# Decoder layer on one core: attention probabilities packed into 128-column tiles, normalization, clip, mask and q copies moved off VectorE, and a new order of steps

## The chip, the cores and the metric

The kernel runs on one core of one Trainium2 chip. The metric is the device time of one execution in microseconds (us). Single instructions are given in us or, where a row says so, in ns. The engines are TensorE (PE, with its weight loads as PEld), VectorE (DVE), ScalarE (ACT), GpSimd (POOL) and SyncE (SP, here only the queue that issues DMAs).

## What is computed

One pre-norm decoder layer for 32 batch rows of 256 tokens with 256 features. Three blocks follow one another, each with a LayerNorm ahead of it and a residual add behind it.

```
x = x + attn(layernorm(x))     # gated slot attention: short convolutions, rope on q and k,
                               # two causal passes with cumulative logsumexp weights
x = x + xattn(layernorm(x), ctx, mask)
x = x + ffn(layernorm(x))      # 8 experts of width 64, top 2, SwiGLU, all experts computed

# xattn: 16 heads of 16 features, 77 context positions
scores = jnp.einsum('bhqd,bhkd->bhqk', Q, K) / scale
scores = jnp.where(mask, scores, NEG_INF)
attention = jax.nn.softmax(scores, axis=-1)
heads_out = jnp.einsum('bhqk,bhkd->bhqd', attention, V)
```

## The kernel before

**Pipeline over batch rows.** A step of the loop works on four batch rows at once: `N` on the newest row (projections, convolution and gates of attn), `A` on the one before (the two passes and the output of attn), `X` on the next (xattn) and `F` on the oldest (ffn). 35 steps bring 32 rows through; names begin with `a_`, `x_` or `f_` by block. Steps 5 and on are an instruction loop of two steps a turn, since most buffers exist twice, by the parity of the row.

**Order.** Every engine has its own list of the parts of a step, written out by hand in `body`, and runs it strictly in order. Parts wait on one semaphore for each result (`on.x_prob`, `on.x_pT` and so on), so an engine stands still at the first part whose operands are late, with all behind it. `A1`, `X0` and the like are names of eight PSUM banks; `E0` carries everything of the projections, `X0` scores and projections of xattn, `X1` transposed probabilities, `X2` the output of the multiply with V.

**Numbers in halves.** Most multiplies take each operand as a rounded part and a remainder (`hi`, `lo`) and are three matmuls. Those of the probabilities, of V, of E and of the small states take four-byte data in one statement, which TensorE runs as two load and multiply pairs.

**xattn.** A row has two chunks of 128 tokens (`c`), and a chunk four groups of four heads (`q`), eight units `u` in all. For each: `x_s` writes scores of 4 x 77 columns to `X0` from block-diagonal masked copies of K (`K_bd`, `KT_lo_bd`, built by GpSimd in `x_kbd`) and adds the mask by a third matmul; `x_soft` on VectorE takes the maximum; `x_prob` on ScalarE makes four exponentials into `prob`; `x_pt` on TensorE transposes them, four 128x77 tiles; `x_pt` on ScalarE copies the result to `probT`; `x_av` multiplies each head's 77x128 tile with V and a column of ones (`Vx`, 17 columns a head), whose product with the probabilities is the denominator. `x_o` divides.

**Normalization.** `norm_stats` on VectorE (statistics of two 128x256 tiles, a `hold`, aggregation, plus epsilon), `rstd` on GpSimd (power -0.5), `norm_apply` on VectorE (subtract, multiply). A `hold` is an operation on one column whose result nobody uses; it stands between an operation and one that reads its result.

**DMA.** The sync queue stores the oldest row, then loads x, the context and the mask for new rows, four DMAs a step; each waits in queue order.

## Time and profile before

| | |
|---|---|
| three runs, us | 1811.38, 1815.34, 1818.04; median 1815.34 |
| span of the profiled execution | 1817.2 us |
| its TensorE clock | 0.981 of full speed |
| TensorE, its weight loads | 1666.7 us (92%), 1497.1 us (82%) |
| VectorE | 1496.2 us (82%) |
| ScalarE | 889.4 us (49%) |
| GpSimd | 774.7 us (43%) |
| HBM traffic | 13 GB/s over the span |

The span runs from the first to the last instruction of the one execution that was profiled; no other time of that execution is reported, so its span stands for it. Busy times are sums over the whole span. They say how much an engine has to do, not what a step waits for; the waits and the chain say that. Lengths of matmuls in a timeline overlap by their pipelines, so the cost of one is read from the start of one group to the start of the next.

### The profile page before, as it was taken

Reading aid. Unit: us, or ns where it says so; the run is one execution under the profiler, and the core shown is the slowest. Engines: PE = TensorE matmul, PEld = TensorE weight load, DVE = VectorE, ACT = ScalarE, POOL = GpSimd, SP = SyncE. Lnnn points to the kernel's source line nnn. Section 1 sums busy time; section 2 is a strip of 40 time slices with the busy share of each in tenths; the row PEclk is TensorE's granted clock in tenths of the full one; section 3 lists DMA queues with packets and bytes.
Section 4 is the critical chain, followed back from the end, with each engine's and each line's share of the span. In section 5 each row is a group of like instructions: output and inputs, shape, how many; then the busy total and the mean of one; then the engine's idle time right before and its main releaser. Section 6 shows DMA issues by size and latency. Waiting matters only on the chain.

```text
span 1817.2 us, 36129 instructions
## 1 busy us (share of the span) xinstructions
PE 1666.7 (92%) x12064; PEld 1497.1 (82%) x12064; DVE 1496.2 (82%) x3540; ACT 889.4 (49%) x2351; POOL 774.7 (43%) x809
## 2 busy tenths in 40 slices
PE   3699999999999999999999999999999999999986
PEld 3588888889888888888888988888888888898875
DVE  4778888888888888888888888888888888888652
ACT  2255544455554455555445555444555444555441
POOL 2344444444544444444444454444444444445320
PEclk9899999999999999999999999999999999999887
DMA  4000000000000000000000000000000000000000
GB/s 113 9 9 1 15 15 15 14 14 0 14 14 14 14 14 14 0 14 14 14 14 14 12 2 14 14 14 14 14 0 14 14 14 14 14 10 5 9 7 12
DMA packets 44572, 24.99 MB, mean 14 GB/s; under 512 B 24432, under 2 KB 44528, under 8 KB 44528
## 3 DMA queue, kind: packets, MB, share of 16 engines
q1 hardware_dynamic: 44528, 24.43, 5.1%
q8 instruction: 25, 0.41, 0.1%
q14 instruction: 19, 0.16, 0.0%
HBM read 16.03 MB, written 8.39 MB: 13 GB/s over the span
## 4 chain that ended last, share of the span: by engine, by line
PE 56%; DVE 30%; issue 9%; ACT 4%; DVEq 0%; DMA 0%; SPq 0%; POOL 0%; ACTq 0%; POOLq 0%
PE bank L377 49%; DVE a_conv L809 6%; PE bank L611 4%; DVE x_nmax L942 3%; DVE dve_scrap L252 2%; DVE a_xn L759 2%; PE bank L383 2%; DVE f_xn L759 2%; ACT x_prob L1211 2%; DVE a_E L792 1%; DVE a_stats L746 1%; DVE x_stats L746 1%; DVE f_s L1018 1%; DVE f_th L1013 1%; DVE x_xnT_lo L774 1%
## 5 line engine op out<-in xcount | busy, mean ns | idle before, releaser
L1211 ACT ACTIVATE x_prob<-bank,x_nmax 128x77 f32<-128x77 f32 x1024 | 247.7, 327 | 167.9 <-DVE x_nmax L942 163.7
L377 PEld LDWEIGHTS bank<-x_Vx,x_probT 77*128 77x128 f32 x2048 | 251.6, 193 | 2.9
L377 PE MATMUL bank<-x_Vx,x_probT 77*128 77x17 f32 x2048 | 246.2, 255 | 0.0
L1222 ACT ACTIVATE x_probT<-bank 77x512 f32<-77x512 f32 x256 | 152.4, 595 | 92.0 <-PE bank L611 92.0
L942 DVE TENSOR_REDUCE x_nmax<-bank 128x4 f32<-128x308 f32 x256 | 121.3, 474 | 59.8 <-PE bank L377 58.4
L611 PE MATMUL bank<-ident,x_prob 128*77 128x128 f32 x1024 | 155.9, 275 | 0.4 <-ACT x_probT L1222 0.4
L809 DVE SCALAR_TENSOR_TENSOR a_conv<-a_raw,cw,a_conv 128x256 f32<-128x256 f32 x384 | 156.2, 477 | 0.0
L1306 POOL TENSOR_TENSOR x_rstd<-x_ve,mhalf 128x2 f32<-128x2 f32 x32 | 22.6, 706 | 301.2 <-DVE x_ve L752 301.2
L1330 POOL TENSOR_TENSOR a_Er_lo<-a_E,a_Er_hi 128x512 fp32r<-128x512 f32 x32 | 74.2, 2320 | 142.2 <-ACT a_Er_hi L1114 142.2
L611 PEld LDWEIGHTS bank<-ident,x_prob 128*77 128x77 f32 x1024 | 124.0, 148 | 7.6 <-issue 0.6
L377 PE MATMUL bank<-x_K_bd,x_Q_stack 128*128 128x308 f32 x256 | 98.6, 385 | 15.0 <-ACT x_prob L1211 12.3
L841 DVE RECIPROCAL a_rC<-bank 128x512 f32<-128x512 f32 x32 | 107.1, 3348 | 0.3 <-PE bank L377 0.3
L1355 POOL TENSOR_TENSOR a_okn<-a_okn,a_okmax 128x512 f32<-128x512 f32 x32 | 33.4, 1043 | 165.0 <-DVE a_okmax L860 165.0
L1377 POOL TENSOR_TENSOR x_K_bd<-x_K_stack,groupmask 128x308 fp32r<-128x308 f32 x128 | 95.1, 771 | 17.5 <-DVE x_KT_lo L916 17.5
L1395 POOL TENSOR_TENSOR f_s<-f_s,f_wt 128x512 f32<-128x512 f32 x64 | 66.8, 1044 | 69.4 <-DVE f_s L1018 69.4
L252 DVE TENSOR_TENSOR dve_scrap<-mhalf 128x1 f32<-128x1 f32 x192 | 83.3, 434 | 5.5
L844 DVE TENSOR_TENSOR a_AT<-bank,tri 128x512 f32<-128x512 f32 x128 | 84.6, 680 | 2.4 <-PE bank L377 2.4
L1363 POOL TENSOR_TENSOR a_orinv<-a_ove,mhalf 128x8 f32<-128x8 f32 x32 | 52.7, 1647 | 79.1 <-DVE a_ove L878 79.1
L1137 ACT ACTIVATE a_ET<-bank 128x512 f32<-128x512 f32 x32 | 19.1, 597 | 133.4 <-PE bank L383 133.4
L1200 ACT ACTIVATE x_Q_stack<-bank 64x512 fp32r<-64x512 f32 x64 | 37.9, 592 | 86.3 <-PE bank L377 85.9
L377 PE MATMUL bank<-x_negmask,ident_bf 128*128 128x308 bf16 x256 | 79.5, 311 | 0.0
L377 PE MATMUL bank<-fwo_hi,f_sT_hi 128*128 128x256 f32 x256 | 76.7, 300 | 1.5 <-ACT f_sT_hi L1251 1.5
(250 smaller groups left out, 5585.2 us busy)
## 6 DMA issues: line engine op xcount, KB each, us to landing
x<-in_x SPq DMA_DIRECT2D x32, 256.0 KB, 2.9
out<-x SPq DMA_DIRECT2D x32, 256.0 KB, 2.2
ctxT<-in_ctxT SPq DMA_DIRECT2D x32, 77.0 KB, 2.5
keep<-in_mask SPq DMA_DIRECT2D x32, 19.2 KB, 2.6
f_s<-in_fWu SPq DMA_DIRECT2D x2, 256.0 KB, 5.6
a_AT<-in_Wv SPq DMA_DIRECT2D x1, 256.0 KB, 3.8
a_okn<-in_Ws SPq DMA_DIRECT2D x1, 256.0 KB, 3.9
a_qn<-in_Wg SPq DMA_DIRECT2D x1, 256.0 KB, 3.8
```

What stands on the lines that cost most here:

```text
L252: eng.tensor_tensor(scrap[:], mhalf[:, 0:1], mhalf[:, 0:1], ALU.mult)
L377: return pe.matmul(out, lhsT, rhs, start=start, stop=stop, skip_group_check=True)
L611: ins = pe.transpose(X1[0:S2, i * P:(i + 1) * P], prob[:, u % 2, i, :], ident[:])
L759: ins = ts(xn[s][:, c, :], src[:, c, :], ln_mv[s][:, c, 0:1], ln_rstd[s][:, c:c + 1], ALU.subtract, ALU.mult)
L809: stt(conv[:, j, :], raw[:, j, i:i + T], cw[:, j, i:i + 1], conv[:, j, :], ALU.mult, ALU.add).then_inc(on.a_conv, 1)
L841: dve.reciprocal(flat(rC[r.parity]), E0[:, :]).then_inc(on.a_rC, 1)
L844: return tt(dst, src.rearrange("p (h t) -> p h t", h=H), tri.rearrange("p (o t) -> p o t", o=1).broadcast_to([P, H, P]), ALU.mult)
L942: dve.tensor_reduce(nmax[:, u % 2, :], X0[:, 0:UH * S2].rearrange("p (h s) -> p h s", h=UH), AX.X, ALU.min).then_inc(on.x_max, 1)
L1211: ins = act.activation(prob[:, u % 2, i, :], X0[:, i * S2:(i + 1) * S2], ACT.Exp, scale=-1.0, bias=nmax[:, u % 2, i:i + 1])
L1222: act.activation(probT[:, u % 2].rearrange("p h t -> p (h t)"), X1[0:S2, :], ACT.Copy).then_inc(on.x_pT, 1)
L1330: pool.tensor_tensor(E_halves[1][:], E[r.parity][:], E_halves[0][:].bitcast(F32), ALU.subtract).then_inc(on.a_Elo, 1)
L1377: pool.tensor_tensor(K_bd[:, q], K_stack[:, q:q + 1, :].bitcast(F32).broadcast_to([P, UH, S2]), spread(groupmask[:], S2), ALU.mult)
```

## The change

**Probabilities packed.** `prob` becomes one array of 16 heads with a pitch of 80 columns, 1280 columns, the three between heads zero. A chunk's 1280 columns are ten tiles of 128, in groups of 2, 3, 2 and 3 tiles as heads become ready (`GROUPS`). Transposes, copies and the multiply work on tiles. V is laid out in blocks to fit (`Vbd`, two of them, 128 x 10 x 51): the rows of a tile belong to two or three heads, and each head has its own 17 columns, with zeros and the ones loaded once. The products add up in one PSUM bank.

```diff
-                for i in range(UH):
-                    ins = pe.transpose(X1[0:S2, i * P:(i + 1) * P], prob[:, u % 2, i, :], ident[:])
+                for i, t in enumerate(GROUPS[u % QU]):
+                    ins = pe.transpose(X1[:, i * P:(i + 1) * P], prob[:, t * P:(t + 1) * P], ident[:])
...
+                    pe.wait_ge(vbd_in, upto(r, V_DMAS))
...
-                for i in range(UH):
-                    h = q * UH + i
-                    ins = mm(X2[:, h * (HD + 1):(h + 1) * (HD + 1)], probT[:, u % 2, i, :], Vx[:, h, :])
+                for t in GROUPS[q]:
+                    h, w = first_head(t) * (HD + 1), tile_heads(t) * (HD + 1)
+                    ins = mm(X2[:, h:h + w], probT[:, t, :], Vbd[r.parity][:, t, 0:w], start=(t == 0),
+                             stop=(t == NT - 1))
```

**V spread by DMA.** ScalarE's `x_v` writes V to `Vtok` (77 x 16 x 16), and the sync queue copies it to its places in `Vbd`, twelve DMAs a row, behind the loads of a step and ahead of the store.

```diff
+            def spread_v(r):
+                sp.wait_ge(on.x_v, upto(r))
+                if second(r):
+                    sp.wait_ge(on.x_av_ps, upto(two_before(r), NU))
+                dst, src = Vbd[r.parity], Vtok[:].rearrange("s (g h) e -> s g h e", g=2)
+                for s, n, h, t, p, col in V_PIECES:
+                    sp.dma_start(dst[p:p + n, t::NT // 2, col:col + HD], src[s:s + n, :, h, :]).then_inc(vbd_in, 16)
```

**Work moved off VectorE.** `norm_apply` becomes two ScalarE activations that scale by `rstd` and add a shift; VectorE makes the negated mean, GpSimd the shift. The clip of the scores ahead of the exponential becomes one behind it, on GpSimd, in place. The mask (`negmask`) is made by GpSimd behind `x_kbd`, the four q copies (`a_qbd`) by ScalarE.

```diff
+                for c in range(TC):
+                    ins = act.activation(xn[s][:, c, :], src[:, c, :], ACT.Identity,
+                                         scale=ln_rstd[s][:, c:c + 1], bias=ln_shift[s][:, c:c + 1])
...
+                pool.wait_ge(on.rstd[s], upto(r))
+                pool.tensor_tensor(ln_shift[s][:], ln_neg[s][:], ln_rstd[s][:], ALU.mult).then_inc(on.shift[s], 1)
...
+            def a_clip(r):
+                pool.wait_ge(on.a_Eraw, upto(r))
+                hold_pool(pool, 1)
+                e = E[r.parity][:].rearrange("p c d -> p (c d)")
+                pool.tensor_scalar(e, e, E_MIN, E_MAX, ALU.max, ALU.min).then_inc(on.a_E, 1)
```

**Other forms of small operations.** A `hold` on VectorE and four small operations become `scalar_tensor_tensor` where they were `tensor_tensor`; one hold goes.

```diff
-            eng.tensor_tensor(scrap[:], mhalf[:, 0:1], mhalf[:, 0:1], ALU.mult)
+            dve.scalar_tensor_tensor(dve_scrap[:, k:k + 1], mhalf[:, 0:1], 1.0, mhalf[:, 0:1], ALU.mult, ALU.mult)
```

**Order.** All engines but SP get new lists. The first parts of xattn (`x_k`, `x_v`, `x_turn`, `x_q`) and of the passes (`a_ktok`, `a_A`, `a_state`) move from the start of a step to the end of the one before; `a_et` moves ahead of `a_wo`. One line of TensorE's list:

```diff
-                X(x_ot); F(f_yy); X(x_proj); N(a_et); N(a_vtok)
+                A(x_v); N(a_ktok); N(a_A, 0); A(x_turn); N(a_A, 1); N(a_state); A(x_q)
```

TensorE late in a step, from the multiply with V of unit 4 on, before. `bank<-x_Vx,x_probT` is the multiply with V, `bank<-ident,x_prob` the transposes; one row of the list is one statement, which for four-byte data is two instructions on the chip.

```order
L619 REGISTER_ALU
L377 MATMUL bank<-x_Vx,x_probT 128x17 x4
L611 MATMUL bank<-ident,x_prob 77x128 x4
L377 MATMUL bank<-x_Vx,x_probT 128x17 x4
L383 MATMUL bank<-ident,a_o 128x128 x4
L604 REGISTER_ALU
L611 MATMUL bank<-ident,x_prob 77x128 x4
L688 MATMUL bank<-ident,f_s 128x128 x4
L377 MATMUL bank<-x_Vx,x_probT 128x17 x8
```

The same place in the change:

```order
L670 REGISTER_ALU
L427 MATMUL bank<-x_Vbd,x_probT 128x34
L427 MATMUL bank<-x_Vbd,x_probT 128x51
L661 MATMUL bank<-ident,x_prob 128x128 x2
L427 MATMUL bank<-x_Vbd,x_probT 128x34
L427 MATMUL bank<-x_Vbd,x_probT 128x51
L427 MATMUL bank<-x_Vbd,x_probT 128x34
L433 MATMUL bank<-ident,a_o 128x128 x4
L654 REGISTER_ALU
L661 MATMUL bank<-ident,x_prob 128x128 x3
L427 MATMUL bank<-x_Vbd,x_probT 128x34
L427 MATMUL bank<-x_Vbd,x_probT 128x51
```

Four transposes for four heads became two or three, and four multiplies two or three, wider ones; the transposes of `a_o` stand where they stood.

TensorE at the end of a step, from the last matmul of `x_proj` on, before (`a_E` is `a_et`, `a_qkv` is `a_vtok`, `ctxT,xwk` is `x_k`, `x_xn` is `x_turn`, `f_xn` and `a_xn` the other two turns):

```order
L377 MATMUL bank<-xwp_hi,x_oT_lo 128x256
L383 MATMUL bank<-ident,a_E 128x128 x4
L465 MATMUL bank<-ident,a_qkv 128x128 x4
L557 ISA
L377 MATMUL bank<-ctxT,xwk 128x77 x4
L474 MATMUL bank<-ident,a_qkr 128x128
L377 MATMUL bank<-a_q_bd,a_qkr 128x512
L377 MATMUL bank<-xwv,ctxT 77x256 x2
L383 MATMUL bank<-ident,x_xn 128x128 x4
L377 MATMUL bank<-a_q_bd,a_qkr 128x512
L493 REGISTER_ALU
L377 MATMUL bank<-a_E,a_ktok 128x256
```

The same place in the change:

```order
L427 MATMUL bank<-xwp_hi,x_oT_lo 128x256
L607 ISA
L427 MATMUL bank<-ctxT,xwk 128x77 x4
L427 MATMUL bank<-xwv,ctxT 77x256 x2
L524 MATMUL bank<-ident,a_qkr 128x128
L427 MATMUL bank<-a_q_bd,a_qkr 128x512
L433 MATMUL bank<-ident,x_xn 128x128 x4
L427 MATMUL bank<-a_q_bd,a_qkr 128x512
L543 REGISTER_ALU
L427 MATMUL bank<-a_E,a_ktok 128x256
L427 MATMUL bank<-a_vtok,a_E 128x128 x2
```

`a_et` and `a_vtok` are gone from here (they stand ahead of Wo and of `x_proj`), and `x_v` stands ahead of the first `a_A`.

The sync queue in the loop, before, from the wait ahead of a store on:

```order
L345 ISA
L345 DMA out<-x_0 128x2x256
L321 ISA
L321 DMA x_0<-in_x 128x2x256
L326 ISA
L326 DMA ctxT<-in_ctxT 128x2x77
L328 DMA keep<-in_mask 128x2x77
```

The same place in the change, where the list goes on with four more DMAs into `x_Vbd`:

```order
L392 DMA out<-x_0 128x2x256
L358 ISA
L358 DMA x_0<-in_x 128x2x256
L363 ISA
L363 DMA ctxT<-in_ctxT 128x2x77
L365 DMA keep<-in_mask 128x2x77
L371 ISA
L374 DMA x_Vbd<-x_Vtok 77x2x16
L374 DMA x_Vbd<-x_Vtok 48x2x16
L374 DMA x_Vbd<-x_Vtok 29x2x16
L374 DMA x_Vbd<-x_Vtok 77x2x16
L374 DMA x_Vbd<-x_Vtok 16x2x16
```

Behind the three loads stand a wait for `Vtok` and the twelve copies, ahead of the next store.

## Rows read from the trace of the kernel before

**Rows 1.** Busy time by engine in four steps: us, busy (xinstructions), PEclk, DMA, GB/s
```profile
774.70:988.40 213.70, 203.21 (x1510) 183.41 (x1509) 186.07 (x440) 109.93 (x292) 96.62 (x100) 1.00 0.04 12
```

**Rows 2.** SP timeline: first and last store in the loop: start, length, queue, line
```profile
185.11 0.38 SPq L345 DMA_DIRECT2D out<-x  x1
...
1685.73 0.39 SPq L345 DMA_DIRECT2D out<-x  x1
```

**Rows 3.** Chain of work in one step: start, length, engine, what
```profile
828.63 0.69 DVE x L961
...
838.20 10.55 PE bank L377 x76
```

**Rows 4.** TensorE timeline, transposes of x_prob and multiplies with V
```profile
801.03 0.60 PE L611 MATMUL bank<-ident,x_prob 128*77 128x128 f32 x4
801.47 0.96 PE L377 MATMUL bank<-x_Vx,x_probT 77*128 77x17 f32 x8
802.28 0.36 PE L377 MATMUL bank<-wg_hi,a_xnT_hi 128*128 128x256 f32 x1
...
808.71 1.00 PE L377 MATMUL bank<-a_vtok,a_AT 128*128 128x64 f32 x8
```

**Rows 5.** Groups of instructions on VectorE, by form, 800 to 1311 us
```profile
L252 DVE TENSOR_TENSOR dve_scrap<-mhalf 128x1 f32<-128x1 f32 x55 | 24.6, 447 | 1.6
...
L759 DVE TENSOR_SCALAR a_xn<-x,a_mv,a_rstd 128x256 f32<-128x256 f32 x18 | 13.4, 785 | 0.0
...
L834 DVE COPY a_q_bd<-a_qkr 32x256 f32<-32x256 f32 x40 | 11.3, 283 | 0.4
...
L792 DVE TENSOR_SCALAR a_E<-bank 128x512 f32<-128x512 f32 x10 | 6.8, 678 | 0.0
...
L759 DVE TENSOR_SCALAR x_xn<-x,x_mv,x_rstd 128x256 f32<-128x256 f32 x18 | 6.6, 411 | 0.0
```

**Rows 6.** Timelines of VectorE and of GpSimd, one step
```profile
801.90 4.83 DVE L809 SCALAR_TENSOR_TENSOR a_conv<-a_raw,cw,a_conv 128x256 f32<-128x256 f32 x12
...
845.29 1.02 DVE L252 TENSOR_TENSOR dve_scrap<-mhalf 128x1 f32<-128x1 f32 x1
...
805.44 2.42 POOL L1330 TENSOR_TENSOR a_Er_lo<-a_E,a_Er_hi 128x512 fp32r<-128x512 f32 x1 [4.47 <-ACT a_Er_hi L1114]
...
845.25 1.04 POOL L1355 TENSOR_TENSOR a_okn<-a_okn,a_okmax 128x512 f32<-128x512 f32 x1 [5.00 <-DVE a_okmax L860]
```

**Rows 7.** GpSimd timeline, masked copies of K
```profile
834.91 2.98 POOL L1377 TENSOR_TENSOR x_K_bd<-x_K_stack,groupmask 128x308 fp32r<-128x308 f32 x4 [0.51 <-DVE x_KT_lo L916]
837.85 2.40 POOL L1380 TENSOR_TENSOR x_KT_lo_bd<-x_KT_lo,headmask 128x616 fp32r<-128x616 f32 x2
```

**Rows 8.** The page's costliest groups, first row (1024 exponentials)
```profile
L1211 ACT ACTIVATE x_prob<-bank,x_nmax 128x77 f32<-128x77 f32 x1024 | 247.7, 327 | 167.9 <-DVE x_nmax L942 163.7
```

**Rows 9.** SP timeline, two loads one behind the other
```profile
829.36 0.37 SPq L326 DMA_DIRECT2D ctxT<-in_ctxT  x1
829.85 0.40 SPq L328 DMA_DIRECT2D keep<-in_mask  x1
```

**Rows 10.** The page's DMA issues: count, KB each, us to landing
```profile
keep<-in_mask SPq DMA_DIRECT2D x32, 19.2 KB, 2.6
```

**Rows 11.** TensorE timeline: Wo, a_v transposes, first and third scores
```profile
822.23 0.36 PE L377 MATMUL bank<-wo_hi,a_oT_hi 128*128 128x256 f32 x1
...
829.87 0.63 PE L465 MATMUL bank<-ident,a_qkv 128*128 128x128 f32 x4 [0.84 <-ACT a_ET L1137]
...
842.67 0.38 PE L377 MATMUL bank<-x_K_bd,x_Q_stack 128*128 128x308 f32 x1
...
850.42 0.30 PE L377 MATMUL bank<-x_K_bd,x_Q_stack 128*128 128x308 f32 x1
```

**Rows 12.** VectorE timeline, f_out
```profile
827.26 0.69 DVE L1027 TENSOR_TENSOR x<-bank,x 128x512 f32<-128x512 f32 x1 [0.95 <-PE bank L377]
```

**Rows 13.** Busy time by engine while only keep lands, last columns DMA share, GB/s
```profile
831.50:832.00 0.50, 0.50 (x2) 0.15 (x1) 0.47 (x4) 0.49 (x2) 0.17 (x1) 1.00 0.41 46
```

More of the change, by code:

```diff
@@ L39 @@
 QU = NH // UH
+PITCH = 80
+NT = NH * PITCH // P
+GROUPS = (range(0, 2), range(2, 5), range(5, 7), range(7, 10))
+VW = 3 * (HD + 1)
 NU = TC * QU
@@ L342, in body @@
                     load_context(ra)
+                if rx is not None:
+                    spread_v(rx)
                 if rf is not None:
```

282 lines of the change are left out of this document (172 added, 110 removed).

## The prediction

> **What bounds the kernel now.** I read the busy time of a steady stretch first, then the steps of the loop on the DMA queue, then the chain of work, then TensorE's own timeline. Four steps of the loop take 213.70 us, 53.4 us each, and in them TensorE is busy 203.21 us, that is 50.8 us a step, VectorE 46.5, ScalarE 27.5 and GpSimd 24.2, at full clock [rows 1]. So TensorE idles 2.6 us a step. The loop is regular: the first and the last store in it are 28 steps and 1500.62 us apart, 53.6 us a step, and the other 316.6 us of the span are filling and draining the pipeline [rows 2]. The chain that ended last alternates: it runs through TensorE for stretches such as 10.55 us, but between the add of x2 at 828.63 and the x_q matmuls at 838.20 it runs through VectorE, 9.6 us of statistics, masks and normalizations [rows 3]. VectorE is therefore a second bound, hidden under TensorE except at the start of a step. A saving on TensorE counts in full only if VectorE, whose queue is 87% full, becomes lighter too. Both happen here.
>
> **Part 1, packed probabilities on TensorE.** Four transposes of 77 columns take 0.44 us from start to start, 0.11 each; eight weight-load and matmul pairs for four heads of V take 0.81 us, 0.101 each [rows 4]. The multiply of four-byte data counts two instructions for one in the code. A batch row has 2 chunks x 16 heads = 32 transposes and 64 of these instructions; it will have 2 x 10 = 20 and 40. The new multiply has 128 rows of weights and 34 or 51 moving columns; the nearest rows are the old 77x17 and a 128x128 weight with 64 columns, a_vtok by a_AT [rows 4]. By their lengths, 1.00 against 0.96 for eight, the new ones are some 0.005 longer; I take 0.105. The stage falls from 6.5 to 4.2 us, 2.3 less; the transposes lose 12 x 0.11 = 1.3. Sum: **3.6 us of TensorE per row**. The bounds are narrow, 3.4 to 3.8.
>
> **Part 2, work that leaves VectorE.** Six normalizations of 128x256 at 0.411 (x_xn, undisturbed) to 0.785 (a_xn, disturbed), about 3.3 us with the overlap between two of them; the clip 0.68; four q copies, 1.1; with the mask of 154 columns, for which I take as much as for the clip, 5.7 us a step [rows 5]. There are six tiny holds a step, 0.447 each, 2.7 us; one goes and the rest become another operation, which I price at 0.16: 1.9 us less [rows 5]. What is added (three negations and smaller pieces) is 0.3. VectorE goes from 46.5 to about 39. Alone this is worth nothing, since TensorE is over it; it pays for letting TensorE's saving through.
>
> Why the holds are long is seen in one of them: a 128x1 operation took 1.02 us beside GpSimd's a_okn, and both ended together. The scalar_tensor_tensor of the convolution, with two SBUF inputs too, kept 4.83 us for twelve while GpSimd's a_Er_lo ran, 0.40 each before and after it began [rows 6]. So the new form of the hold should not wait. The Trainium skill (SBUF — State Buffer, SBUF: two separate sides) says that a VectorE instruction with two SBUF inputs is shut out while GpSimd reads SBUF. By that rule the 1.9 us would stay on VectorE and it would need 41 us, still under TensorE; the convolution's rows speak against it for this form, and the time forecast is the same.
>
> **Part 3, what ScalarE and GpSimd get.** ScalarE: the six normalizations and four q copies at some 0.35 us, 3.5 us, less 1.3 for narrower copies of probT; 27.5 becomes 29.7, with 17 us free. GpSimd gets a clip of 128x512 (a_okn of the same size took 1.04 [rows 6]; 0.9 to 1.3), a mask, a hold and three small products: 24.2 becomes about 27. Neither is a bound in sum; each can be late at one place. The place is GpSimd's masked copies of K, 2.98 + 2.40 us in a row [rows 7], which must end before the first scores.
>
> **Part 4, V spread by DMA.** New on the sync queue: twelve DMAs a row, each 13 to 77 partitions with two runs of 64 bytes. They wait for Vtok, which ScalarE evacuates behind the first x_prob, about 3 us after the first scores start: the scores themselves and a_okn ahead of the maximum, 1.3; the maximum, 0.5; four exponentials of 0.33 that overlap, 1.0 [rows 8]; and the copy. Two loads were issued 0.49 us apart [rows 9], so the twelfth is issued at 3.0 + 11 x 0.49 = 8.4. keep took 2.6 us to land [rows 10]; these pieces are fewer and shorter, and I take 2.2 as an estimate, so V is there at 10.6. TensorE now goes from the first scores at 842.67 to the third at 850.42, 7.75 us [rows 11]; in the new order the third scores, a second group of transposes and the four of a_qn come before the first x_av too, 1.4 more by the same spacing (4 x 0.11 for each group of four). So it is at x_av at 9.2 and stalls; I take **1.4 us a row**. The queue's next item, the store of the row before, is due 25 us later, so nothing behind the twelve is hurt. The bounds: 0 if a DMA inside SBUF lands faster than one from outside, and 5 if packets cost more than I think (first rival).
>
> **Part 5, the new order.** From the first Wo matmul (822.23) to the first scores (842.67) TensorE took 20.4 us. Most of the step's 2.6 us of idle time lies in it, I take 2.3, 0.84 of them for the evacuation of a_ET [rows 11]. a_et now stands ahead of a_wo and a_vtok behind f_yy, so this wait has 5 us of cover and goes. What is late next: f_out can start 5.0 us after Wo began (827.26 [rows 12] against 822.23); behind it in VectorE's queue stand the aggregate for x and x_ve, then GpSimd's power, then ScalarE, whose queue has a_vtok, a_qbd and x_k ahead of x_xn. Going through the four queues with the trace's durations, x_turn is late by 0.2 us, a_state by 0.7 (its mask on VectorE stands behind a_stats, which waits for the x load issued only after f_out's store), x_ql and the K copies by 0.3. That is 1.2 us of idle where 2.3 stood, with bounds 0 and 3. In the rest of the step 0.3 was idle and I leave 0.3: from the third scores on, the maximum, the 4.83 us convolution, the maximum and the exponentials take as long as TensorE's work there, so no surplus remains, but no debt either.
>
> **Sum.** A step: 50.8 of work less 3.6 is 47.2; idle 1.4 + 1.2 + 0.3 = 2.9; 50.1 against 53.4, **3.3 us less**. Over 28 steps 92; the four rows in the filling and draining save the 3.6 of work each, 14, and the lighter start of a step gives there perhaps 2 us in each of six steps, 12. Total 118: the profiled 1817.2 becomes 1699. The median of the runs, 1815.34, is 0.1% under the profiled span, so I forecast **1698 us**.
>
> **Rivals.**
> V late. The packets may queue. A DMA's completion needs its slowest engine. The traffic in 831.50 to 832.00, keep alone, was 0.41 of 0.5 us on 16 engines for 23 KB in pieces of 77 bytes, 11 ns a packet [rows 13]. The Trainium skill (DMA: Bandwidth & Descriptors, Why a DMA increments its semaphore by 16 and not by 1) says that a DMA from this queue uses the largest number of engines up to 16 that divides both outer sizes: 29 and 61 partitions then go to one engine. As a mechanism of this kernel: if one engine gets those two DMAs whole (58 and 122 packets) and its share of the others, some 264 packets, it is busy 2.9 us at 11 ns and stays under the issue time: no change. At three times that it needs 8.7 us, V lands near 14 and the stall is about 5, 3.6 more a row: 1698 + 32 x 3.6 = 1813. Chance 0.12, over 1750 to 1813.
>
> Slower. The same place decides the sign: the gain of 3.3 a step is used up when V lands later than 9.2 + 1.4 + 3.7 = 14.3 us after the first scores. Landing at 18 would add 7.4 x 32, to 1935. Nothing in the trace shows packets that slow, but it shows none between two places in SBUF either. Chance 0.07.
>
> TensorE packed. If V lands in time and the queues at the start of a step overlap better than I can work out, idle falls to about 1.0 and a step takes 48.2: 1817 - 28 x 5.2 - 26 = 1645. For it: VectorE has 7 us more room than before. Chance 0.22, over 1625 to 1665.
>
> A slack chain elsewhere. VectorE or GpSimd late (K copies, conv, the long reciprocal ahead of a_et and a_wo) by 1.5 us more than I have: 1745. Chance 0.12.
>
> The packed form doesn't save: the new pairs cost 0.16 instead of 0.105, and 2.2 us of the 3.6 are lost: 1770. The 64-column rows speak against it. Chance 0.03.
>
> The forecast case, 1665 to 1730, has 0.44.
>
> **Numbers.** The range leaves out the slower case, most of the late V and the best edge: 1640 to 1775. 0.5% of this kernel, 9 us, is about what a measurement can tell from no change. Faster by more than that 0.89, within it 0.03, slower 0.08.
>
> **What would show it.** Right: x_Vbd multiplies about 0.105 us apart, 40 a row; a step of 50 us; TensorE waiting for a DMA into x_Vbd once a row, 1 to 2 us; the wait for a_ET gone; holds at 0.16. Wrong: the x_Vbd wait above 4 us, or absent; TensorE's idle time a step above 4 us with VectorE or GpSimd named; more than 48 us of TensorE work.

## The result, and the profile after

The changed kernel takes 1930.39 us (1929.22 to 1943.56) against 1815.01; taken over all its runs it is 1.066 times as long, 95% interval 1.063 to 1.068. The forecast was 1698, in 1640 to 1775. It is slower, and 155 us over the range's upper end.

Four steps of the loop, from store to store, in the view by windows (PE busy, PEld, DVE, ACT, POOL, then granted clock, share of DMA time, GB/s), the counterpart of [rows 1]:

```profile
767.78:999.84 232.06, 204.14 (x1366) 179.77 (x1366) 158.48 (x401) 124.38 (x333) 110.39 (x124) 0.93 0.06 12
```

A step is 58.0 us where it was 53.4 [rows 1]. VectorE did get lighter, 39.6 us for 46.5. TensorE is busy 51.0 us a step, but at a mean granted clock of 0.93 where it had 1.00 [rows 1]. So two things have to be explained: 7.0 us a step in which TensorE has nothing to do, and the slower clock.

TensorE's waits, by what ended them (us in total, times, longest):

```profile
PE bank L427 <- DMA x_Vbd<-x_Vtok: 120.8, 26, 4.7
...
PE bank L427 <- DVE a_AT L883: 28.0, 27, 3.7
PE bank L433 <- ACT x_xn L1156: 17.4, 22, 1.6
PE bank L427 <- ACT x_prob L1305: 16.8, 35, 2.0
```

The largest is for V; with some 30 us at the same place that have no releaser named it is 151 us, 4.7 a row. Here is one row of it: the sync queue's copies as one line of the timeline (start, duration of the twelve issues), then TensorE's first scores and its first product with V (in brackets the idle time ahead of it and what ended it).

```profile
842.08 9.92 SPq L374 DMA_DIRECT2D x_Vbd<-x_Vtok  x12
```

```profile
839.14 0.30 PE L427 MATMUL bank<-x_K_bd,x_Q_stack 128*128 128x308 f32 x1
...
853.20 1.09 PE L427 MATMUL bank<-x_Vbd,x_probT 128*128 128x34 f32 x4 [4.66 <-DMA x_Vbd<-x_Vtok]
```

The copies start 2.9 us after the first scores, as forecast (3.0). TensorE is ready for them 9.4 us after the first scores, as forecast (9.2). But an issue takes 0.83 us at the median (637 to 1065 ns over all 384), not the 0.49 of [rows 9], so twelve take 9.92 us. The last is issued at 851.13 and lands 2.02 us later, at 853.15 (2.2 was forecast); that is 14.0 us after the first scores, and TensorE waits 4.66 us, not 1.4.

The same place by windows of 2 us (columns as above):

```profile
848.00:850.00 2.00, 0.54 (x3) 0.10 (x1) 1.50 (x4) 1.71 (x4) 0.81 (x3) 1.00 0.07 7
850.00:852.00 2.00, 0.00 (x0) 0.00 (x0) 0.00 (x0) 0.00 (x0) 1.98 (x2) 1.00 0.11 10
852.00:854.00 2.00, 0.81 (x4) 0.81 (x5) 0.00 (x0) 0.00 (x0) 0.00 (x0) 0.79 0.05 5
854.00:856.00 2.00, 2.00 (x10) 1.82 (x10) 0.75 (x2) 0.24 (x2) 0.00 (x0) 0.50 0.00 0
...
860.00:862.00 2.00, 2.00 (x8) 1.52 (x8) 0.48 (x2) 0.00 (x0) 2.00 (x2) 0.50 0.00 0
862.00:864.00 2.00, 2.00 (x10) 1.72 (x10) 1.10 (x3) 1.49 (x5) 1.25 (x2) 0.65 0.00 0
864.00:866.00 2.00, 2.00 (x21) 2.00 (x19) 0.67 (x1) 0.17 (x1) 0.45 (x1) 1.00 0.00 0
```

TensorE does nothing from 848.5 to 853.2. Behind it the granted clock is 0.50 for some 10 us, that is 1.2 GHz in place of 2.4, although TensorE is busy throughout. From 854 to 862 it works at half speed and needs 8 us for 4 us of work. The prediction had no term for this.

VectorE's groups of the convolution and of the holds (busy us in total, mean ns of one):

```profile
L857 DVE SCALAR_TENSOR_TENSOR a_conv<-a_raw,cw,a_conv 128x256 f32<-128x256 f32 x384 | 158.1, 488 | 11.5 <-POOL a_conv L1428 11.5
...
L284 DVE SCALAR_TENSOR_TENSOR dve_scrap<-mhalf 128x1 f32<-128x1 f32 x160 | 26.2, 164 | 3.5
```

The holds are 0.164 us each, as forecast, against 0.447 [rows 5]. The convolution's mean of 488 ns is near the 477 of the kernel before, so here it is undisturbed; that changes below.

### The profile page after: what moved, and what is told of

Read it like the earlier page. It is cut to its first block, busy times and chain, and to the rows that moved or that the text cites. A ratio compares the mean times of both kernels' runs of the same rounds, so it can differ in the third digit from the quotient of the medians.

```text
span 1929.0 us, 34569 instructions
## 1 busy us (share of the span) xinstructions
PE 1636.6 (85%) x10912; PEld 1436.2 (74%) x10912; DVE 1283.8 (67%) x3220; ACT 1003.4 (52%) x2671; POOL 883.1 (46%) x1001
## 4 chain that ended last, share of the span: by engine, by line
PE 33%; issue 16%; DVE 13%; POOL 13%; SPq 12%; ACT 7%; DMA 6%; DVEq 0%; ACTq 0%; POOLq 0%
PE bank L427 27%; SPq L374 12%; PE bank L433 3%; DMA x<-in_x 3%; DMA x_Vbd<-x_Vtok 3%; POOL a_orinv L1466 3%; POOL pool_scrap L288 2%; ACT x_prob L1305 2%; POOL a_E L1418 2%; POOL a_qkr L1440 2%; POOL a_conv L1446 2%; POOL f_s L1500 2%; DVE x_nmax L983 1%; DVE x_Q_stack L972 1%; PE bank L740 1%
## 5 line engine op out<-in xcount | busy, mean ns | idle before, releaser
L427 PE MATMUL bank<-x_Vbd,x_probT 128*128 128x34 f32 (+1 forms) x1280 | 190.3, 284 | 151.4 <-DMA x_Vbd<-x_Vtok 120.8
L427 PEld LDWEIGHTS bank<-x_Vbd,x_probT 128*128 128x128 f32 x1280 | 186.0, 213 | 165.4 <-DMA x_Vbd<-x_Vtok 132.1
L288 POOL TENSOR_TENSOR pool_scrap<-mhalf 128x1 f32<-128x1 f32 x64 | 64.7, 1012 | 244.5 <-ACT a_E L1200 202.3
L1316 ACT ACTIVATE x_probT<-bank 128x256 f32<-128x256 f32 (+1 forms) x256 | 113.8, 444 | 28.7 <-PE bank L661 28.7
L427 PE MATMUL bank<-x_K_bd,x_Q_stack 128*128 128x308 f32 x256 | 107.6, 420 | 18.0 <-ACT x_prob L1305 16.8
L661 PE MATMUL bank<-ident,x_prob 128*128 128x128 f32 x640 | 120.6, 289 | 0.9 <-ACT x_probT L1316 0.9
L661 PEld LDWEIGHTS bank<-ident,x_prob 128*128 128x128 f32 x640 | 87.5, 155 | 5.8 <-ACT x_prob L1305 1.2
L427 PE MATMUL bank<-x_KT_lo_bd,x_Q_stack 128*128 128x308 f32 x256 | 84.1, 329 | 0.0
L427 PEld LDWEIGHTS bank<-x_K_bd,x_Q_stack 128*128 128x128 f32 x256 | 54.1, 211 | 38.0 <-ACT x_prob L1305 26.1
L427 PE MATMUL bank<-a_qn_bd,a_ET 128*128 128x256 f32 x256 | 76.7, 427 | 0.3 <-ACT a_qn_last L1253 0.3
L1483 POOL TENSOR_TENSOR x_KT_lo_bd<-x_KT_lo,headmask 128x616 fp32r<-128x616 f32 x64 | 76.8, 1221 | 0.0
```

What stands on the lines that cost most here:

```text
L288: pool.tensor_tensor(pool_scrap[:, k:k + 1], mhalf[:, 0:1], mhalf[:, 0:1], ALU.mult)
L427: return pe.matmul(out, lhsT, rhs, start=start, stop=stop, skip_group_check=True)
L661: ins = pe.transpose(X1[:, i * P:(i + 1) * P], prob[:, t * P:(t + 1) * P], ident[:])
L1316: act.activation(probT[:, g[0]:g[-1] + 1, :].rearrange("p h t -> p (h t)"), X1[:, 0:len(g) * P], ACT.Copy).then_inc(on.x_pT, 1)
```

## The experiments

All times are medians; ratios are to the kernel before on the same chip. The runs came from four chips, on which the kernel before took 1813.7 to 1816.1 us, so a difference between two of them is good to some 3 us beside their own spread.

| kernel | what it is | us | ratio, 95% interval |
|---|---|---|---|
| early_v | changed, V evacuated earlier | 1847.2 | 1.018 (1.017 to 1.020) |
| no_copies | changed, no V copies | 1850.3 | 1.020 (1.018 to 1.022) |
| rows80 | changed, V pieces of 16n partitions | 1843.3 | 1.015 (1.010 to 1.020) |
| unpacked | changed, packing undone | 1984.5 | 1.092 (1.089 to 1.095) |
| pack_only | before, with packing alone | 1810.7 | 0.998 (0.997 to 0.999) |
| pause1 | before, TensorE held 1.8 us a row | 1942.5 | 1.069 (1.063 to 1.074) |
| pause2 | before, TensorE held 3.5 us a row | 2049.1 | 1.132 (1.127 to 1.136) |
| clip_dve | early_v, clamp on VectorE | 1838.6 | 1.015 (1.013 to 1.017) |
| split | early_v, x_soft 4 within a_conv | 1770.2 | 0.976 (0.973 to 0.978) |
| split_clip | both | 1762.2 | 0.971 (0.967 to 0.974) |
| masks | split_clip, a_maskP earlier too | 1725.5 | 0.952 (0.948 to 0.955) |
| masks_a | masks, a_maskA 0 earlier | 1732.8 | 0.955 (0.953 to 0.958) |
| masks_x1b | masks, GpSimd's xbias add earlier | 1724.9 | 0.951 (0.949 to 0.953) |
| masks_late | masks, V late again | 1907.1 | 1.052 (1.049 to 1.056) |
| masks_unp | masks, packing undone | 1866.2 | 1.029 (1.026 to 1.032) |
| pack_split | pack_only, x_soft 4 within a_conv | 1834.4 | 1.011 (1.009 to 1.013) |
| pack_masks | pack_split, a_maskP earlier too | 1778.8 | 0.981 (0.978 to 0.984) |

### V in time: early_v, no_copies, rows80

ScalarE evacuates V as soon as it can instead of behind the first x_prob:

```diff
-  X(x_xn); A(a_ktok); X(x_xnt)
+  X(x_xn); A(a_ktok); X(x_v); X(x_xnt)
...
-  X(x_prob, 0); X(x_v); F(f_gap)
+  X(x_prob, 0); F(f_gap)
```

> The change, with one part of ScalarE's list moved: the copy of V into Vtok stands behind a_ktok at the start of a step, no longer behind the first x_prob, so the twelve DMAs start some 13 us earlier; nothing is added or removed. Theory (late V): in the change TensorE stood 4.6 us a row at the first x_av for these DMAs, and its granted clock was 0.50 for the 10 us behind that. Both go: 32 x (4.6 + about 5) = 307 us less than 1930, so 1625 to 1690. Rival (the clock falls for another reason, such as the waits at the start of a step): only the wait goes, 32 x 4.6 = 147, about 1780. Rival (the DMAs disturb something by being there, wherever they stand): above 1850.

1847.2: the wait for V is gone and 83 us with it. That is about a third of the 240 to 305 that the theory wanted, and less than the 147 of the wait alone. The waits say where the rest went:

```profile
PE bank L427 <- ACT x_prob L1305: 85.1, 37, 2.8
```

The waits ahead of the first product with V were 151 us in the changed kernel. They are gone, and the wait for x_prob has grown from 16.8 to 85.1 us. The difference, 83 us, is the whole gain. The mean granted clock is 0.926 in both: the stretch at half clock didn't go, it moved behind the new wait.

no_copies issues no copy at all and waits for none; the multiplies read blocks without V, so its output lacks the attention to the context.

> The change without the twelve DMAs of a row and without the waits for them: V never gets into its blocks (they hold zeros and the ones), so the attention's output leaves V out; every instruction of the engines stays. Theory (late V): as fast as the kernel with V early, within 10 us, 1625 to 1690, since DMAs that are in time cost nothing. Rival (the copies cost also by occupying the sync queue ahead of the load of x and by DMA traffic): faster than the kernel with V early by more than 20 us.

1850.3, within 3 us of early_v. Once V is in time, the 384 copies cost nothing that can be told from no change. What is left, 35 us over the kernel before and 150 over the forecast, is not V.

rows80 leaves V at its late place and cuts the pieces at multiples of 16 partitions (zero rows fill up to 80).

```diff
-                while s < S2:
+                while s < PITCH:
                     t, p = divmod(h * PITCH + s, P)
-                    n = min(S2 - s, P - p)
+                    n = min(PITCH - s, P - p)
```

> The changed kernel, V copied at its place, but in pieces that begin and end at multiples of 16 partitions (80 rows a head instead of 77, still 12 copies of the same shape otherwise). The copies of 13 to 77 partitions take 0.83 us each to issue (637 to 1065 ns) where the loads of whole tiles take 0.4. If uneven counts of partitions cost the issue, the spacing falls to 0.65 or less, V lands 2 us sooner, and of the 4.6 us wait 2.5 is left: 1860 to 1890. If it is the number of descriptors (rows x 2 heads), it stays at 0.83 and the time at 1930.

The twelve issues, and TensorE's wait:

```profile
810.82 7.93 SPq L374 DMA_DIRECT2D x_Vbd<-x_Vtok  x12
```

```profile
819.98 1.00 PE L427 MATMUL bank<-x_Vbd,x_probT 128*128 128x34 f32 x4 [2.67 <-DMA x_Vbd<-x_Vtok]
```

An issue is 0.615 us at the median, the wait 2.67 us instead of 4.66, the time 1843.3 (1833.3 to 1853.3): 87 us less, for 2.0 us a row, and less than the 1860 to 1890 that was expected. More bytes in the same number of copies are issued faster. And though TensorE still waits 2.67 us a row for V, the kernel is no slower than early_v, where it doesn't wait at all: in this order the last part of V's delay costs nothing. The mean of its convolution, 496 ns, is still that of an undisturbed one, and the section on the middle of a step shows why that matters.

The Trainium skill (DMA: Bandwidth & Descriptors, Why a DMA increments its semaphore by 16 and not by 1) says that a copy goes to the largest number of engines up to 16 that divides its outer sizes, one for 29 or 61 partitions, 11 for 77, 16 for multiples of 16. The trace agrees that the count of partitions matters, but what it shows is a shorter issue, 0.83 to 0.615 us. It does not show the number of engines as the reason. In the order of the list (77, 48, 29, 77, 16, 61, 64, 13, 77, 32, 45 and 77 partitions) the twelve issues of the changed kernel from 842.08 on take 0.91, 0.65, 0.72, 0.91, 0.65, 0.68, 0.81, 0.88, 0.84, 0.65, 0.86 and 0.86 us. The long ones are those of 77, 13, 45 and 64 partitions, while the two that by the page go to one engine, 29 and 61, are issued in 0.72 and 0.68. What makes an issue long stays open. The prediction had weighed the rule only for the time of the DMA engines, and so had put it aside.

### What a stall of TensorE costs: pause1, pause2

To the kernel before, with nothing else changed, one copy of 128 words inside SBUF is added for every row, and TensorE waits for it ahead of its first product with V. pause2 has two, the second issued when the first has landed.

```diff
+            def pause(r):
+                sp.wait_ge(on.x_pT_ps, upto(r, NU, 2))
+                sp.dma_start(pause_to[:, 0:0+1], mhalf[:, 0:1]).then_inc(pause_in, 16)
...
                 if u == 0:
                     pe.wait_ge(on.x_v, upto(r))
+                    pe.wait_ge(pause_in, upto(r, 16))
```

> The kernel before, with one thing added: when TensorE has transposed the second piece of probabilities, SyncE copies 128 words within SBUF and TensorE waits for it ahead of the first product with V. It does nothing but hold TensorE for one transfer, about 2.1 us a row at that place. Theory one, a stall of TensorE costs its own length: 32 x 2.1 = 67 us over the kernel before, 1882. Theory two, it costs more, as the granted clock falls to half for some us behind it: 1930 or more. Theory three, it costs less, as the other engines catch up in it and the waits of the kernel before (a_xn, f_xn, x_prob: 70 us) shrink: 1840 or less.

> The same with two such copies, one behind the other, so about 4.3 us a row, near the 4.6 that TensorE waited for V in the changed kernel. Its own length: 32 x 4.3 = 138 us, 1953. With half a clock for 8 us behind it (the changed kernel's trace shows 0.50 from 853.6 to 863.3), which costs 4 us more a row: 2060 to 2080. With catching up: 1900 or less.

pause1 around one such wait, windows of 2 us:

```profile
906.00:908.00 2.00, 2.00 (x18) 1.81 (x16) 1.74 (x3) 1.64 (x6) 2.00 (x4) 1.00 0.00 0
908.00:910.00 2.00, 0.27 (x3) 0.23 (x3) 1.97 (x4) 0.59 (x1) 1.53 (x2) 1.00 0.04 0
910.00:912.00 2.00, 2.00 (x18) 1.91 (x18) 0.75 (x3) 0.17 (x1) 0.00 (x0) 0.95 0.00 0
912.00:914.00 2.00, 2.00 (x12) 2.00 (x10) 2.00 (x6) 1.95 (x7) 0.00 (x0) 0.50 0.00 0
914.00:916.00 2.00, 2.00 (x11) 2.00 (x11) 2.00 (x6) 1.94 (x5) 0.00 (x0) 0.50 0.00 0
916.00:918.00 2.00, 2.00 (x10) 1.91 (x10) 0.62 (x2) 0.92 (x2) 1.71 (x1) 0.50 0.00 0
918.00:920.00 2.00, 2.00 (x11) 1.65 (x10) 0.46 (x2) 0.27 (x1) 0.00 (x0) 0.84 0.00 0
```

TensorE's waits at this place sum to 56.8 us over the 32 rows in pause1 and to 109.6 in pause2, 1.8 and 3.4 us a row. The kernel lost 127 and 233 us, so every microsecond of stall cost 2.2 and 2.1 on the average. The second microsecond is the clock: 1.7 us without work at 908, and from 912 to 918 the granted clock is 0.50 with TensorE fully busy. Over the whole execution the mean clock falls from 0.981 to 0.940 and 0.912. Against the kernel before that is 82 and 145 us of lost clock, and with the stalls 139 and 255, somewhat over the loss. A part of the surplus has a name: the wait for x_prob, 12.3 us in the kernel before, is 1.9 in both, so some 10 us were covered by the pauses. Theory two held, with a little of theory three. The Trainium skill (TensorE: Matmul & The Clock Gate, HAM oscillation — how this bites in real kernels) tells of a kernel whose TensorE falls to half its clock after each wait for a DMA. The traces agree, with the rows above. But not every wait of this length does it. In masks, a kernel of a later section, a wait of 1.97 us for a_AT that ends at 745.89 is followed by 0.54 and 0.60 in the windows from 746 to 750, while behind this one it is 1.00 as far as 900:

```profile
848.40 0.70 PE L427 MATMUL bank<-a_E,a_ktok 128*128 128x256 f32 x2 [1.80 <-DVE a_AT L889]
```

### Packing against order: unpacked, pack_only

unpacked keeps the new order (ScalarE's x_v at its late place too) and the work moved off VectorE, and has the old transposes and products.

> The change with the old form of probabilities, transposes, copies of probT and V (Vx, no Vbd, no DMAs); the work moved off VectorE and the new order stay. Theory: TensorE has the 3.6 us a row back, and no wait for V, so 32 x 3.6 = 115 us above the kernel with V early: 1740 to 1800, at or a little under the 1815 of before. Rival (the new order is worse by itself, its waits at the start of a step being longer than before): 1830 or more.

pack_only is the kernel before with the packed tiles and V copied early, in the old order.

> The kernel before with only the packed probabilities, V in blocks and the twelve DMAs, the copy into Vtok placed early in ScalarE's list; VectorE keeps its 46.5 us a step, all lists keep their old order. Theory of the prediction (VectorE is a second bound that must become lighter too): less than the 115 us of TensorE's saving comes through, 1740 to 1790. Rival (TensorE's saving comes through alone): 1700. Rival (packing itself costs): above 1815.

1984.5 and 1810.7. The order and the moved work together cost 170 us (1984.5 against 1814), and no run parts the two; packing in that order earns 137 (unpacked against early_v), yet in the old order it earns 4. The same transposes and products were saved both times. In pack_only TensorE waits 49.6 us, in 36 pieces, for the x_prob behind the convolution, where the kernel before waited 12.3; in all, TensorE's idle time grew from 150 to 216 us while its busy time fell from 1667 to 1593.

### The middle of a step: clip_dve, split, split_clip, masks

In early_v VectorE runs all twelve a_conv between x_soft 3 and x_soft 4 (VectorE, then TensorE, then windows):

```profile
811.96 7.94 DVE L857 SCALAR_TENSOR_TENSOR a_conv<-a_raw,cw,a_conv 128x256 f32<-128x256 f32 x12
819.82 0.47 DVE L983 TENSOR_REDUCE x_nmax<-bank 128x4 f32<-128x308 f32 x1
```

```profile
821.34 0.63 PE L427 MATMUL bank<-x_K_bd,x_Q_stack 128*128 128x308 f32 x1 [2.79 <-ACT x_prob L1305]
```

```profile
818.00:820.00 2.00, 0.55 (x6) 0.42 (x4) 2.00 (x4) 0.00 (x0) 0.82 (x1) 1.00 0.00 0
820.00:822.00 2.00, 0.66 (x2) 0.50 (x2) 1.67 (x4) 1.68 (x6) 0.00 (x0) 0.66 0.00 0
822.00:824.00 2.00, 2.00 (x11) 1.98 (x10) 1.91 (x6) 2.00 (x7) 0.29 (x1) 0.50 0.00 0
```

The convolution takes 7.94 us, where it took 4.83 [rows 6]. x_soft 4 stands behind it, ScalarE's x_prob 4 behind that, and TensorE, which needs x_prob 4 to have X0 free, waits 2.79 us at 821.34 and then runs at 0.50. It is the same pair of costs as with V. The late V had hidden it. The changed kernel, VectorE and then GpSimd:

```profile
855.25 0.48 DVE L983 TENSOR_REDUCE x_nmax<-bank 128x4 f32<-128x308 f32 x1 [5.70 <-PE bank L427]
855.64 4.83 DVE L857 SCALAR_TENSOR_TENSOR a_conv<-a_raw,cw,a_conv 128x256 f32<-128x256 f32 x12
```

```profile
849.71 1.04 POOL L1500 TENSOR_TENSOR f_s<-f_s,f_wt 128x512 f32<-128x512 f32 x1 [1.19 <-DVE f_s L1080]
850.71 1.26 POOL L1493 TENSOR_TENSOR x<-x,xbias 128x512 f32<-128x512 f32 x1
```

While TensorE stood still VectorE had no scores to work on and stood still too, and GpSimd did f_s and the add of xbias. The convolution came after the stall, with neither beside it, and took 4.83 us; and TensorE, at half clock, had enough to do until x_prob 4 was there.

clip_dve moves the clip of a_E (`a_clip`, called the clamp in what follows) from GpSimd to VectorE between the fourth and the fifth of a_conv. split leaves it on GpSimd, puts x_soft 4 behind the eighth and, on ScalarE, x_prob 4 ahead of a_ehi. split_clip does both.

```diff
 # VectorE, split_clip
-  X(x_soft, 3); N(a_conv); X(x_soft, 4); A(a_maskP, 0); A(a_maskP, 1); N(a_gate)
+  X(x_soft, 3); N(a_conv, 1, 4); N(a_clip); N(a_conv, 5, 8); X(x_soft, 4); N(a_conv, 9, 12);
+  A(a_maskP, 0); A(a_maskP, 1); N(a_gate)
 # ScalarE, split and split_clip
-  X(x_pt, 2); N(a_ehi); X(x_prob, 4); N(a_gt)
+  X(x_pt, 2); X(x_prob, 4); N(a_ehi); N(a_gt)
```

> Against early_v one thing is moved: the clamp of a_E goes from GpSimd back to VectorE, between the first four and the last eight of the twelve a_conv instructions; x_soft 4 stays behind all twelve. In early_v the twelve take 7.94 us a step (mean 709 ns, one up to 1500) where the kernel before had 4.83, and GpSimd's clamp (2.15 us) runs beside them; TensorE then waits 2.8 us for x_prob 4, and its clock falls to half for some 6 us. Theory one, the clamp on GpSimd holds VectorE up: the twelve are back at 4.8 to 5.0 us, x_soft 4 is 2.6 us earlier, the wait for x_prob is under 1 us and the half-clock stretch goes, 32 x (2.6 + 2 to 3) = 150 to 180 us under early_v's 1847: 1670 to 1700. Theory two, only the wait is bought back and the clock is as before: 32 x 2.6 = 83 under, 1765. Theory three, the twelve stay at 7.9 us because something else beside them (the loads, ScalarE) holds them: 1835 to 1855.

> Against early_v the clamp stays on GpSimd; x_soft 4 moves up to between the eighth and the ninth of the twelve a_conv instructions, and on ScalarE x_prob 4 moves ahead of the copy a_ehi, which waits for the clamp (2.9 us a step in early_v). Theory one, the mid-step chain conv, x_soft 4, x_prob 4 costs its wait and the stretch at half clock behind it: the 2.8 us wait for x_prob goes to under 0.5, 1690 to 1740. Theory two, order does not matter and VectorE's total does, since the twelve still take 7.9 us: a_maskP and x_soft 5 become the late ones, 1810 to 1850.

> Both edits: the clamp on VectorE between the fourth and the fifth of a_conv, x_soft 4 between the eighth and the ninth, x_prob 4 ahead of a_ehi. If the two causes are one chain, this gains little over the better of the two (under 15 us), and the waits that are left are those at the start of a step (a_AT 28 us, x_xn 16, x 9): 1660 to 1700. If they are separate (VectorE's time beside GpSimd, and the order), they add: each one's gain over early_v summed. If the packed kernel on this chip is bound by something that neither touches, both stay above 1800.

clip_dve's convolution in two pieces, then GpSimd beside it:

```profile
812.17 3.38 DVE L859 SCALAR_TENSOR_TENSOR a_conv<-a_raw,cw,a_conv 128x256 f32<-128x256 f32 x4
...
815.81 4.29 DVE L859 SCALAR_TENSOR_TENSOR a_conv<-a_raw,cw,a_conv 128x256 f32<-128x256 f32 x8
```

```profile
812.02 1.04 POOL L1500 TENSOR_TENSOR f_s<-f_s,f_wt 128x512 f32<-128x512 f32 x1 [1.20 <-DVE f_s L1086]
813.02 1.45 POOL L1493 TENSOR_TENSOR x<-x,xbias 128x512 f32<-128x512 f32 x1
816.62 1.60 POOL L1433 TENSOR_TENSOR a_Er_lo<-a_E,a_Er_hi 128x512 fp32r<-128x512 f32 x1 [2.15 <-ACT a_Er_hi L1212]
```

The clamp was not what held the convolution up: 7.7 us without it, and theory three of that run is right (1838.6), though what lies beside it is GpSimd's other work, not the loads or ScalarE; masks_x1b below tests that. The first four take 3.38 us beside f_s and the add of xbias. The order mattered: split gained 77 us. split_clip gained 8 more, about what clip_dve alone had gained (9); the times came to 1770 and 1762, above the ranges expected, because the wait moved on. The largest was now for a_AT, which a_maskP writes, 57.6 us in 44 pieces, since four of a_conv still stood ahead of a_maskP. So masks moves both a_maskP ahead of the last four:

```diff
-  X(x_soft, 4); N(a_conv, 9, 12); A(a_maskP, 0); A(a_maskP, 1)
+  X(x_soft, 4); A(a_maskP, 0); A(a_maskP, 1); N(a_conv, 9, 12)
```

> split_clip (1762) with the two a_maskP instructions moved ahead of the last four of a_conv on VectorE. In split_clip TensorE waits 57.6 us in 44 pieces for a_AT, which a_maskP writes 1.7 us after x_soft 4 because four of a_conv lie between. If that wait has only taken the place of the one for x_prob, it goes: a_AT under 25 us, 1725 to 1740. If the next late thing is x_soft 5 (now 1.6 us later in line for nothing but a_conv), the wait shows up on x_prob again and the time stays at 1755 to 1765.

VectorE in masks, then TensorE's waits, then four steps:

```profile
865.97 3.39 DVE L859 SCALAR_TENSOR_TENSOR a_conv<-a_raw,cw,a_conv 128x256 f32<-128x256 f32 x4
869.28 0.41 DVE L864 TENSOR_SCALAR a_E<-a_E 128x512 f32<-128x512 f32 x1
869.62 1.66 DVE L859 SCALAR_TENSOR_TENSOR a_conv<-a_raw,cw,a_conv 128x256 f32<-128x256 f32 x4
871.21 0.46 DVE L989 TENSOR_REDUCE x_nmax<-bank 128x4 f32<-128x308 f32 x1
871.59 1.27 DVE L889 TENSOR_TENSOR a_AT<-bank,tri 128x512 f32<-128x512 f32 x2
872.79 2.68 DVE L859 SCALAR_TENSOR_TENSOR a_conv<-a_raw,cw,a_conv 128x256 f32<-128x256 f32 x4
```

```profile
PE bank L427 <- ACT x_prob L1311: 25.5, 88, 2.0
PE bank L427 <- DVE a_AT L889: 23.5, 14, 2.1
...
PE bank L433 <- ACT x_xn L1162: 16.7, 21, 1.6
PE bank L740 <- POOL f_s L1500: 13.6, 31, 2.0
```

```profile
688.59:892.66 204.07, 191.61 (x1367) 167.48 (x1366) 169.46 (x405) 124.00 (x333) 96.30 (x116) 0.99 0.06 14
```

1725.5: a step is 51.0 us, TensorE is busy 47.9 of them at a clock of 0.99, and no wait that comes back in the steps is longer than 2.1 us. The moves since early_v, a few items of the written order, are worth 122 us. masks is 4.8% faster than the kernel before, and 27 us over the forecast of the change. That it comes so near is in part luck: the forecast's sum held 1.4 us a step for V, which masks doesn't wait for at all, and 1.5 for the other waits, where masks has 3.1 us of idle time a step.

### Do the parts add: masks_late, masks_unp

> masks (1725.5) with V copied at the changed kernel's own place again, so that the twelve copies land some 10 us after the first scores plus 4 more. Nothing else is late in masks, so the full price of the late V should show: a wait of 4.6 us a row, and by the two pauses (127 us for 32 x 1.8, 233 us for 32 x 3.5) about 2.1 times its length, 32 x 4.6 x 2.1 = 310 us: 2035. By the 83 us that it cost in the changed kernel, where other waits took its place once it was gone: 1810. By its own length: 1872.

> masks with the packing undone: 16 transposes of 77 columns and 16 x 2 products a row as before, no copies of V, the new order and the work moved off VectorE kept. TensorE then has 3.6 us a row more to do: if it is what bounds masks, 32 x 3.6 = 115 over 1725.5, 1840. As unpacked against early_v (137 us): 1862. If the rest of masks is bound elsewhere, 1725 to 1760.

masks_late takes 1907.1: the late V costs 182 us here and cost 83 in the changed kernel. Its wait (4.66 us) is the same. Read the other way, the mended order is worth 122 us with V early and 23 with V late. The two stalls stand in the same half of a step and one covers the other. None of the three numbers in the expectation was right. The waits at this place sum to 152 us (120.6 of them with the DMA named), and the mean clock of 0.929 against 0.970 loses 83 us more; of these 236 us, 54 came back. Some 26 of them are waits that shrank: that for x_prob from 25.5 to 6.5 us and that for x_probT from 8.1 to 0.9. The other 28 lie in the clock's term: TensorE's busy time grew by 52 us (1562.3 to 1614.6), not by 83. In pause2 the waits of the kernel before for a_xn, a_ET and f_xn, far from the pause in a step, stayed as they were, and that for x_prob, the next behind it, all but went. So a stall covers the one that lies close behind it.

masks_unp takes 1866.2: packing is worth 141 us, 4.4 a row, where nothing is late. That is more than the 3.6 us of TensorE's work, which itself came out as forecast: over the four steps of masks shown above, transposes and products with V take 25.5 us from start to start with waits left out, in the kernel before 40.0, so 3.6 us less a row, and a product is 0.105 us behind the last. The rest of the 4.4 is clock and waits: the mean clock of masks_unp is lower, 0.945 against 0.970, and it waits 51.5 us in 24 pieces, with no releaser named, ahead of transposes of a_xn and f_xn. And without packing, the mended order and the moved work still cost 52 us against the kernel before.

### The old order once more: pack_split, pack_masks

> pack_only (packing alone in the order of before, 1810.7) with x_soft 4 between the eighth and the ninth a_conv. There TensorE waits 49.6 us in 36 pieces (up to 2.1) for x_prob, each the one behind a_conv. If that wait is where the packing's saving went: the 1.5 us a step and part of the half clock behind it come back, 1730 to 1765. If VectorE (83% busy) is the bound as a whole, its later work (a_maskP, x_soft 5) is late by what x_soft 4 gained and the time stays within 10 us of 1811.

> pack_split (1834), whose wait had moved to a_AT (51.1 us in 31 pieces), with both a_maskP ahead of the last four of a_conv. If the step is bound by when VectorE hands x_soft 4 and a_maskP over, the wait goes and the time falls under pack_only's 1811, to 1750 to 1780. If VectorE's total (83% busy) binds, it stays at 1800 to 1830, with the wait on x_soft 5's x_prob.

pack_split was slower than pack_only, by 24 us: the wait for x_prob was traded for one for a_AT,

```profile
PE bank L420 <- DVE a_AT L891: 51.1, 31, 2.0
```

and pack_masks took that away and came to 1778.8, 32 us under pack_only. So what held the time at 1811 was which item stood behind the convolution, and not VectorE's total of 83% alone. Of the 115 us of the packing's saving, 35 have come through here. masks, with a lighter VectorE and the rest of the new order, is 53 us faster still; which of these two gives the 53 was not tried.

### Two that gained nothing: masks_a, masks_x1b

masks_a moves a_maskA 0 behind f_stats; masks_x1b moves, on GpSimd, the add of xbias ahead of a_tap0.

> masks with a_maskA 0 moved on VectorE from behind the second mean and variance to behind f_stats, at the start of a step. In masks TensorE waits 1.80 us for it (848.40) in every other step, where its scores were ready at 844.4 and VectorE came to it at 847.65. Theory: the wait of 23.5 us for a_AT goes, and half a clock with it if there is any: 1695 to 1710. Rival: f_ve and so f_xn are 0.6 us later and TensorE waits at f_turn instead, 1720 to 1730.

> masks (1725.5) with one step moved on GpSimd: the add of xbias to x1 (1.45 us) goes ahead of a_tap0, so that of GpSimd's work only f_s (1.04 us) lies beside the first four of a_conv on VectorE. In masks these four take 3.39 us where four elsewhere take 1.66, with f_s and the add beside them from 865.83 to 868.29. Theory one, GpSimd's instructions with two operands in SBUF hold VectorE's up: the four fall to 2.2 to 2.7 us, mean of all twelve under 0.56 (now 0.60), and the time by 0 to 25 us, as TensorE waits little there: 1700 to 1725. Theory two, the first four are long for another reason (they follow a_tap0): they stay at 3.4, 1720 to 1730.

masks_a took 1732.8, 7 us more and outside both ranges: the wait of 1.80 us for a_AT became one of 2.05 us for x_xnT_lo, whose place in VectorE's queue it had taken. masks_x1b took 1724.9, no change. But the convolution, first four, next four and last four, shows the cause of its length (masks is above, from 865.97; the mean of its twelve was 0.68 us, not the 0.60 that the expectation took from split_clip):

```profile
863.40 2.38 DVE L859 SCALAR_TENSOR_TENSOR a_conv<-a_raw,cw,a_conv 128x256 f32<-128x256 f32 x4
...
866.03 1.66 DVE L859 SCALAR_TENSOR_TENSOR a_conv<-a_raw,cw,a_conv 128x256 f32<-128x256 f32 x4
...
869.20 2.68 DVE L859 SCALAR_TENSOR_TENSOR a_conv<-a_raw,cw,a_conv 128x256 f32<-128x256 f32 x4
```

The first four take 2.38 us in place of 3.39, 1.01 less for 1.45 us of GpSimd's work taken away. The time lies in both ranges, but the first four didn't stay at 3.4, so theory one held for the hold-up, and its price here is nothing, since TensorE waits there only 0.2 us.

## Why the prediction was wrong, step by step

**What bounds the kernel** was read rightly as far as it went: TensorE's idle time was 2.6 us a step and its clock 1.00 in the stretch that I read. That the clock could be lost was not asked, and no term of the sum or of a rival had it.

**Part 1, packing**, was right, mechanism and size: 3.6 us a row forecast and 3.6 measured from start to start, with products 0.105 us apart. In time it was worth more where nothing was late (141 us, 4.4 a row, masks_unp against masks) and next to nothing in the old order (4 us, pack_only). TensorE's work is 47.9 us a step in masks for 47.2 forecast.

**Part 2** was right: VectorE 39.6 us a step for 39, holds 0.164 us for 0.16. Its last clause, that this pays by letting TensorE's saving through, was not. A total under TensorE's is no proof; the order in which VectorE hands things over decided 122 us.

**Part 3** had GpSimd's total right (27.6 us for 27) and its danger in the wrong place, at the copies of K. It was at the convolution, which grew from 4.83 to 7.9 us (early_v) once GpSimd's f_s and add lay beside it. The clip was 1.93 to 2.15 us for 0.9 to 1.3. ScalarE came to 31.1 us a step for 29.7; the 17 us that it was said to have free don't follow from 50.1 less 29.7, which is 20, but nothing rested on them.

**Part 4 is the step that failed first.** "Two loads were issued 0.49 us apart" was carried over to copies of 13 to 77 partitions; these take 0.83. Landing was 14.0 us after the first scores, not 10.6, and the wait 4.66 us, not 1.4. And the wait was priced at its own length, with nothing for the clock behind it. The first rival had the landing (near 14) and the stall (about 5) right, for another reason: slow packets, where it was the issue. Its price of 1813 still left out the clock and the middle of a step, and the kernel took 1930. The second rival's 1935 is near that by luck, since it goes with a landing at 18.

**Part 5** had 0.3 us of idle for the rest of a step, with "no surplus remains, but no debt either" at the convolution. With V in time the debt is 2.8 us a step plus the half clock behind it. The rival on a slack chain had named the convolution, at 1.5 us and with no clock. At the start of a step 1.2 us were forecast; 2.5 stand in every second step of the changed kernel (0.68, 1.56 and 0.22), where VectorE also stands still 3.19 us ahead of the add of x, and 1.3 in the others.

**The sum.** 1930 less 1698 is 232 us. V in time takes 83 of them (early_v), the middle of a step 122 (early_v to masks), and 27 are left with masks, whose step is 51.0 us for the 50.1 forecast. That is one order of taking them away; in the other the middle is 23 and V 182. The terms don't add, because both are stalls of TensorE, each with a stretch at half clock behind it, and they hide one another: late V took away the wait for x_prob, and once V was in time that wait and its stretch at half clock came in V's place.

Open: why TensorE's busy time in masks_late grew by 31 us less than its lost clock, why one wait of 1.8 us costs the clock and another doesn't, why TensorE in masks_unp has a lower clock than in masks, what makes a copy's issue long, and what the work moved off VectorE and the new order are worth each by itself. No run has one without the other.

## What to carry to other kernels

When an order written by hand is changed, go through the queue of the engine that feeds the bound and ask of each long item what stands behind it; splitting one item, the convolution, and moving a few short ones was worth 122 us here, where the lighter VectorE and all the rest of the new order together are worth 53 (pack_masks to masks). Look at the clock in the windows behind a stall of TensorE before you price it: in the two pauses a stall cost twice its length, and in masks the clock stayed whole behind one of the same length. And undo or mend one part at a time in both directions: the late V hid the convolution, and the convolution hid a good half of what V was worth (83 us of 182).
